# Transformer block on one core: token sums kept where the tokens lay, value tiles behind the first products, other orders in the last kv head, the last chunks and the experts

## The reference, cut to what matters

```python
x = x + _L0_xattn_ref(_layernorm(x), ctx_4096, ctx_4096, Wq, Wk, Wv, Wd)   # 32 query heads, 8 kv heads of 128, rotary, causal
x = x + _L0_attn_ref(_layernorm(x), Wq, bq, Wk, bk, Wv, bv, Wo, bo)        # 32 heads of 16, causal, biases
x = x + _L0_ffn_ref(_layernorm(x), W_base, b_base, W_gate, W_thr, b_thr, A, B)
```

## Time and profile before

| | |
|---|---|
| runs, median of 3 | 738.43 us (737.69 to 738.82) |
| profiled execution | 738.54 us |
| its span | 736.7 us |
| granted TensorE clock, mean | 0.998 |
| TensorE busy | 710.8 us (96%) |
| VectorE, ScalarE, GpSimd busy | 520.8, 371.9, 485.9 us |

### The profile page before, as it was taken

The page is one execution under the profiler, slowest core; times in us unless marked ns, Lnnn a source line. Parts: engine busy times, 40 slices in busy tenths (PEclk is TensorE's granted clock), DMA queues, the critical chain, the costliest instruction groups (busy, mean ns, idle before and its releaser), DMA issues.

```text
span 736.7 us, 12893 instructions
## 1 busy us (share of the span) xinstructions
PE 710.8 (96%) x4848; PEld 565.4 (77%) x4848; DVE 520.8 (71%) x815; ACT 371.9 (50%) x555; POOL 485.9 (66%) x366
## 2 busy tenths in 40 slices
PE   9999997799999999999999999989999999999897
PEld 7788886567787778787778778767787888877786
DVE  5756857766756757767757757757667887888855
ACT  5456645635544644743653554544246776653220
POOL 1898535678777776867867867746325799964440
PEclk9999999999999999999999999999999999999999
DMA  7553514031211310311301212200200110020003
GB/s 271 206 172 132 172 51 133 17 129 44 86 44 44 107 49 17 113 41 43 100 28 44 98 43 72 73 16 15 87 1 1 44 59 2 2 87 1 15 1 114
DMA packets 25561, 51.09 MB, mean 69 GB/s; under 512 B 2352, under 2 KB 10672, under 8 KB 25520
## 3 DMA queue, kind: packets, MB, share of 16 engines
q1 hardware_dynamic: 25520, 50.53, 20.8%
HBM read 40.04 MB, written 10.49 MB: 69 GB/s over the span
## 4 chain that ended last, share of the span: by engine, by line
PE 79%; DVE 7%; POOL 6%; ACT 3%; issue 3%; DMA 1%; SPq 0%; DVEq 0%; POOLq 0%
PE pj L1517 11%; PE sc L1610 9%; PE pj L1610 9%; PE pj L1708 8%; PE tp L1517 7%; PE pv L1503 6%; PE pv L1597 4%; PE tp L1610 4%; PE sc L1577 3%; PE tp L1491 2%; PE pj L1491 2%; PE sc L1758 2%; PE tp L1584 2%; PE tp L1771 2%; PE pv L1782 2%
## 5 line engine op out<-in xcount | busy, mean ns | idle before, releaser
L482 POOL TENSOR_TENSOR sw<-sw,cst 128x512 f32<-128x512 f32 x72 | 100.6, 1398 | 38.3 <-ACT sw L655 38.2
L1517 PE MATMUL pj<-x,w 128*128 128x512 f32 x384 | 103.5, 406 | 1.0 <-ACT pc L693 0.6
L506 POOL TENSOR_TENSOR sm<-sm,mx 128x512 f32<-128x512 f32 x64 | 72.0, 1131 | 45.5 <-DVE mx L1166 26.4
L1517 PEld LDWEIGHTS pj<-x,w 128*128 128x128 f32 x384 | 69.4, 189 | 24.6 <-DVE cq L1089 4.9
L500 POOL TENSOR_TENSOR w<-raw,w 128x896 fp32r<-128x896 f32 x28 | 60.9, 2196 | 34.6 <-ACT w L640 34.6
L511 POOL TENSOR_TENSOR sm<-sm,rz 128x512 f32<-128x512 f32 x64 | 65.9, 1043 | 19.5 <-DVE rz L1181 19.5
L1517 PE MATMUL tp<-x,w 128*128 128x512 f32 x288 | 76.2, 401 | 2.6 <-ACT sw L655 1.4
L488 POOL TENSOR_TENSOR qr<-t,sw 128x512 f32<-128x512 f32 x54 | 73.3, 1358 | 7.7
L775 ACT ACTIVATE sm<-sm 128x512 f32<-128x512 f32 x64 | 40.2, 631 | 69.2 <-POOL sm L506 69.2
L1708 PE MATMUL pj<-xh,ws 128*128 128x512 f32 x192 | 64.3, 401 | 0.2 <-ACT kb L863 0.2
L1517 PEld LDWEIGHTS tp<-x,w 128*128 128x128 f32 x288 | 51.9, 188 | 13.3 <-ACT sw L655 1.7
(11 more groups left out here) (268 smaller groups left out, 1799.3 us busy)
## 6 DMA issues: line engine op xcount, KB each, us to landing
rawd<-in_w_d SPq DMA_DIRECT2D x16, 512.0 KB, 3.3
raw<-in_w_q SPq DMA_DIRECT2D x15, 512.0 KB, 3.3
kscr<-sm SPq DMA_DIRECT2D x16, 256.0 KB, 2.2
vscr<-sm SPq DMA_DIRECT2D x16, 256.0 KB, 2.6
kr<-kscr SPq DMA_DIRECT2D x8, 512.0 KB, 3.3
vv<-vscr SPq DMA_DIRECT2D x16, 256.0 KB, 2.6
raw<-in_w_k SPq DMA_DIRECT2D x4, 512.0 KB, 6.2
cT<-in_ctxT SPq DMA_DIRECT2D x4, 512.0 KB, 7.4
```

The costliest lines, as they stand in the source:

```text
L482: pool.tensor_tensor(bs(sw[par][:, :]), bs(sw[par][:, :]), rep(cst[:, C_SIN:C_SIN + S], HB), ALU.mult).then_inc(sin_done, 1)
L506: pool.tensor_tensor(s3, s3, per_group(mx[:, c, :], 8), ALU.subtract).then_inc(subbed, 1)
L1517: last = pe.matmul(bank, a, r, start=(start and k == 0 and part == 0), stop=(stop and k == 1 and part == 2), skip_group_check=True)
```

## The change

Five parts:

1. **Token sums where the tokens lay.** `x7` shrinks to 5 blocks. The high and low parts of blocks 5 and 6 are written to a new tensor `xt`, which lies over `cT`, each part onto tokens or sums that are no longer needed. `wdh` and `wdl` lie in the freed space, and a fourth rotation buffer `t1x` takes the place of `pt1` in the first stage.
2. **Value tiles behind the first products.** Tiles 13 to 15 follow the last first product. With that the load of the first keys goes ahead of the last stores of values, `w7_sum(2)` goes behind the rotations, and the rotated parts are added in another order (parts 2 and 3 before 4 and 5), so the first scores wait for six.
3. **Last kv head.** Output tile 5 of head 6 goes ahead of the scores, 6 between them, 7 in two halves around `pv_x(g, 0)`.
4. **Last chunk pairs.** Shares of 8 matmuls a chunk in steps of 4; additions and statistics are separate and earlier; the last `vc_copy` is on ScalarE; `exp` of two chunks goes ahead of `out_hi`.
5. **Third norm and experts.** GpSimd waits for the four normalised tiles before it splits further weights; three bias additions go ahead of the last split, five behind the last normalised tile; `base(5)` is cut around the transposes of the expert activations.

```diff
-        x7 = sb(xs, "x7", [P, 7, 2, 1024], F32R)
+        x7 = sb(xs, "x7", [P, 5, 2, 1024], F32R)
+        wdh = sb(xs, "wdh", [P, REP, D], F32R)
+        wdl = sb(xs, "wdl", [P, REP, D], F32R)
...
+        xt = sb(xs, "xt", [P, KT, TOK], F32R)
...
         def x7b(i, hl):
+            if i >= 5:
+                kh, h = (((1, 1), (0, 1)), ((0, 0), (1, 0)))[i - 5][hl]
+                return xt[:, 2 * kh:2 * kh + 2, h * HALF:(h + 1) * HALF]
...
-        OUT_SHARE = 6
+        OUT_SHARE, OUT_STEP = 8, 4
...
-        t1f, swf = t1 + pt, sw + swx
+        t1f, swf = t1 + [pt[0], t1x], sw + swx
# SyncE
+                if vi == 11:
+                    for i in range(2):
+                        sp.wait_ge(s_ks[i], 16 * NKT // 2)
+                    sp.wait_ge(wlo, 4)
+                    load_kr(0)
             sp.wait_ge(vproj, NVT)
             for i in range(2):
                 load_d(0, i)
+            sp.wait_ge(wlo, 6)
+            load_q(1, 1)
             for i in range(2):
                 sp.wait_ge(s_vs[i], 16 * NVT // 2)
             for i in range(2):
                 load_vv(0, i)
-            sp.wait_ge(wlo, 6)
-            load_q(1, 1)
# GpSimd
-            first_add(2, 4)
-            first_add(3, 5)
+            first_add(2, 2)
+            first_add(3, 3)
...
-            pool.wait_ge(stp, 7 * N_PAIR)
+            pool.wait_ge(outx, 8 * (NKV - 1))
             pool.memset(kb[0][:, :, :, :], 0.0).then_inc(zeroed, 1)
...
             ln_pow(4)
-            for i in range(N_SELF, len(late)):
-                late_lo(i)
+            pool.wait_ge(ln_xn, 2 * NT + 4)
+            late_lo(N_SELF)
+            late_lo(N_SELF + 1)
+            pool.wait_ge(s_row2, 32)
+            for i in range(3):
+                base_bias(i)
+            late_lo(N_SELF + 2)
             ln_pow(5)
-            pool.wait_ge(s_row2, 32)
-            for i in range(NT):
-                pool.wait_ge(ln_xn, 2 * NT + i + 1)
-                pool.tensor_tensor(X[:, i, :], X[:, i, :], brow_b[:, :], ALU.add).then_inc(xbo, 1)
+            pool.wait_ge(ln_xn, 3 * NT)
+            for i in range(3, NT):
+                base_bias(i)
# ScalarE
-                if i == 5:
-                    act.wait_ge(vproj, NVT)
+                if i >= 5:
+                    act.wait_ge(x_done, 5)
...
             first_swap(1, T_BANK)
-            v_copy(13)
+            block_hi(5)
             part_copy(u2, 5, A_BANK)
             part_copy(u2b, 6, B_BANK)
-            v_copy(14)
-            v_copy(15)
-            block_hi(5)
             block_hi(6)
...
             w7_hi(2, 0, raw8, 13)
-            first_swap(6, C_BANK, None, 5)
-            first_swap(7, T_BANK, None, 6)
+            v_copy(13)
+            first_swap(6, C_BANK, None, 3)
+            v_copy(14)
+            first_swap(7, T_BANK, None, 4)
+            v_copy(15)
...
-                    if v == NSU - 2 and c == 0:
-                        out_hi(v - 1)
                     if n + 2 < N_SS:
                         exp(N_SM + n + 2, (n + 2) % 4, S_SCALE)
                         exp(N_SM + n + 3, (n + 3) % 4, S_SCALE)
+                    if v == NSU - 2 and c == 0:
+                        out_hi(v - 1)
+                    if v == NSU - 2 and c == 2:
+                        vc_copy(v + 1)
# VectorE
-            w7_sum(2)
             block_lo(5)
             block_lo(6)
...
                 first_t1(4 + p, a, 1 + p)
-            first_add(4, 2)
+            w7_sum(2)
             c_add(13, 3, C_BANK, u2)
-            first_add(5, 3)
+            dve.wait_ge(cadd, 5)
+            first_t1(6, C_BANK, 3)
+            first_add(4, 4)
+            first_add(5, 5)
+            c_add(14, 4, C2, u2b)
+            dve.wait_ge(cadd, 6)
+            first_t1(7, C2, 4)
             w7_lo(2, 0, 0)
-            c_add(14, 4, C2, u2b)
-            dve.wait_ge(cadd, 5)
-            first_t1(6, C_BANK, 5)
             w7_lo(2, 0, 1)
-            dve.wait_ge(cadd, 6)
-            first_t1(7, C2, 6)
...
-                if 2 * m in (OUT_AT + 2, OUT_AT + 4):
-                    out_add_s((2 * m - OUT_AT - 2) // 2)
-                if c == 2 and v + 1 < NSU:
+                if 2 * m == OUT_AT:
+                    out_add_s(0)
+                elif 2 * m == OUT_AT + 2:
+                    out_add_s(1)
+                    stats_s(0)
+                elif 2 * m == OUT_AT + 4:
+                    stats_s(1)
+                    out_add_s(2)
+                    stats_s(2)
+                if c == 2 and v + 1 < NSU - 1:
# TensorE
             v_tile(12)
-            v_tile(13)
...
-            v_tile(14)
-            v_tile(15)
...
                 product(c, p, W_S4, X_22, False, True).then_inc(stp, 1)
+            for i in range(13, NVT):
+                v_tile(i)
...
-                pe.wait_ge(rope, Q0 + 4 if first else ri(m, 0))
+                pe.wait_ge(rope, Q0 + 6 if first else ri(m, 0))
...
+            out_x(g - 1, 5, O6_BANK)
             pe.wait_ge(rope, Q0 + 8 * NKV)
             pe.wait_ge(s_kr, 16 * NKV)
             scores_x(g, 0, True)
             scores_x(g, 1, True)
-            out_x(g - 1, 5, O6_BANK)
+            added(g - 1, 3)
+            out_x(g - 1, 6, O6_BANK)
             scores_x(g, 2)
             scores_x(g, 3)
             p_transposes(g, 0)
-            added(g - 1, 3)
-            out_x(g - 1, 6, O6_BANK)
-            pe.wait_ge(tp_c, 4 * g + 1)
+            pe.wait_ge(swp, Q0 + 8 * NKV)
+            out_x(g - 1, 7, O6_BANK, end=REP // 2)
+            pv_x(g, 0)
             p_transposes(g, 1)
-            pv_x(g, 0)
-            pe.wait_ge(swp, Q0 + 8 * NKV)
-            out_x(g - 1, 7, O6_BANK)
+            out_x(g - 1, 7, O6_BANK, first=REP // 2)
             pv_x(g, 1)
...
-                if n >= OUT_AT:
-                    at = OUT_SHARE * (n - OUT_AT)
-                    out_s(at // (3 * KT), at % (3 * KT), at % (3 * KT) + OUT_SHARE)
+                for m in range(OUT_SHARE * max(n - OUT_AT, 0), OUT_SHARE * max(n - OUT_AT + 1, 0), OUT_STEP):
+                    out_s(m // (3 * KT), m % (3 * KT), m % (3 * KT) + OUT_STEP)
...
-            out_s(3)
             out_s(4)
...
-            base(5)
+            base(5, end=3)
...
+            base(5, first=3)
```

61 lines of the change are left out of this document (37 added, 24 removed).

## The result

| | us |
|---|---|
| changed kernel, median of 5 runs | 728.98 (725.55 to 730.67) |
| kernel before, median of 5 runs | 738.45 (737.69 to 739.23) |
| ratio of times, 95% interval | 0.9866 (0.9838 to 0.9893) |
| profiled execution, its span | 727.08, 725.3 |

The change makes the kernel 1.3% faster, some 9.5 us. The forecast was 724.5 with a range to 728.5, so the sign and most of the size were right, and the time lies 0.5 us outside the range. The range of the five runs is new: 5.1 us, where before it was 1.5. Their mean granted clocks were 0.998, 0.992, 0.995, 0.995 and 1.000, in the order 727.08, 730.67, 730.03, 728.98, 725.55: the slower a run, the lower its clock. Only the first of them has a trace.

What follows compares the result with a forecast made beforehand. TensorE was busy 710.8 of 736.7 us, so only 26 us of standing, mostly head 0, and clock losses could be won. 7.9 (first stage) + 0 (last head) + 6.1 (tail) = 14.0; 738.5 - 14.0 = 724.5 us, range 722.5 to 728.5.

Steps and rivals of the forecast that it cites:

- So the head moves as the mask does: Head 0: the chain behind the first mask is unchanged, so the head comes earlier by as much as its mask, 7.9 us.
- the scores start at 119.4, without idle time: First stage: TensorE goes from the moved value tiles straight to head 0's scores at 119.4, before at 122.56 after 2.72 idle.
- 130.91 - 122.9 = 8.0 us, of which I count 7.9: First stage: head 0's mask starts at 122.9, not 130.91, a gain counted as 7.9 us, with ends 6.5 and 9.5.
- head 0's length: Sign to check: head 0 takes near 58.8 us, before 63.54; if not, the prediction is wrong first of all.
- the loop heads at 52.7: Sign to check: TensorE's loop heads still take 52.7 us each; if not, the prediction is wrong first of all.
- parts 4 and 5 by 117.2: First stage: VectorE's adds of rotated parts 4 and 5 are done by 117.2, following parts 2 and 3 by 115.9.
- This edit gives 0: the stall only moves: Last kv head: TensorE's wait moves from before the scores to before a pv product, 2.9 us; ends -0.5 and +2.0.
- The tail's 6.1 us: Last chunk pairs, third norm and experts: a base product starts at 695.6, not 701.69, and all behind it moves as one.
- my two steps for it: Tail: 2.7 us for GpSimd waiting for four normalising passes, 1.6 for moving bias adds from beside the second four.
- The clock falls in the last head: Rival 1, chance 0.28: behind the new 2.9 us stall, 3.3 us at half speed cost 1.6, giving 726.1 us.
- a wait of 2 us: Last chunk pairs: part of the gained fill becomes a 2 us wait of TensorE ahead of token tile 4.
- left it at full speed: Argument against rival 1: the 2.10 us idle at 496.11 in the kernel before was followed by full clock.

Runs made afterwards that it cites:

- the last kernel: Two new orders of VectorE (first stage, last kv head) and one of ScalarE, no extra products, against the changed kernel: 723.37 us, ratio 0.9788 to the kernel before.

## Why the prediction was right in part, and where it failed

*"So the head moves as the mask does"* held: from the mask to head 1 it is 55.23 us, 55.19 before. *"the scores start at 119.4, without idle time"* held too: 118.83, of which 0.65 are this execution's early start.

*"130.91 - 122.9 = 8.0 us, of which I count 7.9"* was mis-sized; it measured 6.46, just under the lower end of 6.5 that was given. The prediction's own sign for it, head 0's length, says the same: from its scores to head 1's it is 60.20 us, not 58.8. The other sign, the loop heads at 52.7, held (442.49 - 179.03 over five heads is 52.69). The step that was wrong inside the term is *"parts 4 and 5 by 117.2"*. These two adds of VectorE, with 1.3 us for both, began when forecast (115.36; with this execution's early start of 0.65 added, 116.0 for 115.9), but took 2.63 us, partly beside GpSimd, where the add at 123.16, with GpSimd idle, took 0.69. So the rotation of part 7 behind them came 0.8 us late, and the copy of tile 15 at 120.58, 121.2 on the scale of before, not 119.7. Behind its end the mask came 2.6 us later, as forecast. But that path was only half of it: VectorE's own last add, which began at 123.16, ended just then too. In two of the seven traces with that order the mask waited for the store, by 0.21 and 0.24 us; in the others the rows show no wait between that add and the mask. The run with the order turned round had its copy at 119.9 on the scale of before, all but as forecast, and its mask still 0.8 us late, behind that queue: its weight splits, which the prediction doesn't name, took 3.17 us.

*"This edit gives 0: the stall only moves"* held to 0.05 us, and the run with the old order is as fast. The tail's 6.1 us held: tile 4 came 7.29 us earlier than before, against 5.44 at the start of the stretch, so 1.85 for 1.8; the transposes of hw 11.53, which makes 6.1 for the stretch. The steps between held too: base product 1 starts at 690.24, 6.0 us early for the stretch. GpSimd's order, its wait and its bias additions together, was shown to carry 3.5 us of this in the traces, where my two steps for it add up to 4.3; the other 0.8 us were not tested.

The step that failed is the clock, which the sum 7.9 + 0 + 6.1 puts at nothing and leaves to the first rival, *"The clock falls in the last head"* (0.28), *"726.1 us"*. Its mechanism was right, and its price for a short fall too; its chance and its reach were not. It should have been the main case: in all three traces of kernels that left that wait of 2.78 us empty a fall stood behind it, and in none of those that filled it. It is not certain either: of the 15 runs of these kernels three had a mean clock of 1.000. And it was tied to one place. The same prediction worked out *"a wait of 2 us"* ahead of tile 4 and didn't ask the same question there; the kernel with the old last head falls exactly behind it. The reasoning was that 2.10 us at 496.11 *"left it at full speed"* in one execution of before. One trace without a fall was read as a rule. And the range took the rivals one at a time, where two came together.

Put together: 724.5, plus 1.4 for the first stage, plus 1.6 for a fall in the last head is 727.5 us. The changed kernel's second five runs have their median there (727.45). That it fits to 0.1 us is luck, for the start of the program alone moves by 1.2 us. Of the first five runs, with their median at 728.98, this leaves 1.5 us open; a further fall or a longer one, as seen at a price of 1.5 and 2.9 us, would do it, but no trace of such a run was kept.

The page of the Trainium skill that was named there (TensorE: Matmul & The Clock Gate, What's actually happening) says that the throttled state is the default and activity releases it. The runs agree in direction: with extra products in the two waits all five mean clocks were 1.000, without them they went down to 0.992.

## What to carry to other kernels

When a change only moves a stall, ask what stands behind it: a fall of the clock behind a stall cost about half its length here where the queue of TensorE was full, and nothing where TensorE waited again anyhow. A trace is one draw; a wait of 2 us that kept its clock in it may lose it in the next run, so a time at an even clock and the price of a fall belong in the sum as two terms. And before filling a stall with a better order on the waiting engine, read the two or three instructions that stand ahead of its releaser on the other engines: here turning those round gave the 1.6 us that the reordering of TensorE could not.

## What the runs showed that I had not expected

- Behind the same kind of wait the clock fell for a little over 3 us (cost 1.6 us) or for over 6 us (cost 2.9 us), and in some executions not at all.
- A wait of 1.83 us was enough in one trace (0.50 from 670 to 673 us); in four others the same wait was followed by full clock.
- TensorE's 11 extra products in the wait of the last head did not delay the product behind them: it stands 61.93 and 61.94 us behind the scores of head 6, for 61.95 without them.
- The mean clock of a run also counts the end, where TensorE has nothing left to do: the trace of the last kernel has 0.50 from 721 us on, when the last matmul had ended at 718.5. Small differences of the mean clock are no measure of lost time. Nor was one large one: a run of before with its waits filled had a mean clock of 0.947 and took 740.64 us, 1.9 over the median.
